# A fused attention kernel on one core: copies one step later, a longer routing tail, and the two evacuations of transposed rows moved from ScalarE to VectorE

## The chip, the core and the metric

The kernel runs on one NeuronCore of a Trainium2 chip. The metric is the device time of one launch in microseconds (us). The engines are PE (TensorE), DVE (VectorE), ACT (ScalarE), POOL (GpSimd) and SP (SyncE, which here only issues DMAs). Each runs its own list of instructions in order, and they meet only through semaphores.

## What is computed

Sixteen images of 256 rows with 77 text rows each go through a small transformer block. Cut to what matters:

```python
h = clip(sum(abs(conv2x2(x))), 0, 1)                  # 256 image rows of 256
h = concatenate([h, take(weight, x_txt)], axis=1)      # + 77 text rows: S = 333
n = layernorm(h)
q, k, v = n @ Wq + bq, n @ Wk + bk, n @ Wv + bv        # 16 heads of 16
# windows of 128 rows at stride 64 (4), and a last one: 5 windows
probs = softmax(q_w @ k_w.T * scale + pos_bias)        # per head and window, 128 x 128
merged = scatter_add(probs @ v_w) / counts
h = h + merged @ Wo + bo
x = layernorm(h)
scores, sel = top_k(softmax(x @ gate_w.T), 2)          # 8 experts, 2 for each row
out = h + sum_k(scores * (silu(x @ w1[e]) * (x @ w3[e])) @ w2[e])
```

## The kernel before

The first part (the first 830 us or so of the span) goes over the images with `run_steps`, `b` from -2 to 17. Each engine's `step(b, par)` unrolls `G` = 20 small steps `k` (5 windows of 4 groups, a group being 4 heads). In step `k` of image `b`:

- PE computes the scores of group `k` (L1026), transposes the probabilities of group `k-3` (L1040) and multiplies those of group `k-4` with v (L1063).
- DVE adds the bias and takes the row minimum (L757), ACT takes the exponent (L622), and the transposed probabilities are copied out of `t_bank` by ACT (L636, three groups of four) or DVE (L772, the fourth). `probs` has 4 buffers, `probsT` and the score bank 2.

Between these, at numbers of `k` written out by hand on every engine, stands the work for other images: projection for image `b+1` (`proj`), input and first layernorm of `b+2` (`inp`), output projection, second layernorm and transposes of `b-1` (`tail`), and the routing to experts of `b-2` (`tail2`). Since each engine is in order, a place in this order decides what waits behind what.

The projection matters most. ACT writes q and k to `qk` (L660). Each is then split in three bf16 parts: DVE makes the first (`part_high`, L733), POOL the remainder (`split_rest`, L502), DVE the second (`part_middle`, L738), POOL the third (`split_last`, L507). The argument 0 is q, 1 is k. SP writes the parts to DRAM (`write_part`, L366) and reads them back six times over as the stacks from which the scores are computed (`load_stack`, L372: 6 DMAs for q, 6 for k, 166.5 KB each). SP's order, for the projection of image `b+1`, is written out: the parts q0, k0, q1, q2, k1 (10 DMAs), then the q stack, then k2 (2 DMAs), the store of h, the k stack, and the four shifts of v. The k stack waits until all parts of k have landed. PE's first score matmul of the next image waits for both stacks.

The routing ends in six scatters of rows into expert regions (`scatter`, L493), issued from POOL.

The second part (from about 883 us on) is the expert stage, 91 tiles.

Of the kernel before, what the change touches and what calls it, by code (L numbers as in the profile page):

```python
# [29 lines left out]
GH = 4  # L30
# [28 lines left out]
def build(nc, x, x_txt, table, Wq, bq, Wk, bk, Wv, bv, Wo, bo, pos_bias, gate_wT, w1, w2, w3, use, out):  # L59
    ctx = ExitStack()  # L60
    with ctx:
# [72 lines left out]
        probsT = sb("probsT", [P, 2, GH * WIN])  # L134
# [182 lines left out]
        def _(sp):  # L317
# [17 lines left out]
            def step(b, par):  # L335
# [24 lines left out]
                if proj:  # L360
# [49 lines left out]

            sp.wait_ge(wo_done, B * 2)
# [24 lines left out]
        def _(pool):  # L436
# [50 lines left out]
            def step(b, par):  # L487
# [22 lines left out]
                for k in range(G):  # L510
                    v = (k - 5) // NG
                    if (k - 5) % NG == 3 and ((att and v >= 0) or (tail and v < 0)):
# [9 lines left out]
                    if inp and k == 0:  # L522
                        pool.wait_ge(idx_in, b2 * 16 + 16)
# [3 lines left out]
                        pool.indirect_dma_start(h_in[par][0:TXT, 2, :], None, table,  # L527
                                                bass.IndirectOffsetOnAxis(text_idx[0:TXT, 0:1], 0)).then_inc(text_in, 16)
                    if inp and k == 2:
                        pool.wait_ge(x_in, b2 * 64 + 64)  # L530
                        if b2 >= 1:
                            pool.wait_ge(image_ready, b2)
                        pool.tensor_tensor(diag[:, :, :], x_here[:, :, 0:IMG], x_below[:, :, 1:IMG + 1],
                                           ALU.subtract).then_inc(diffs_ready, 1)
                    if inp and k == 3:
                        pool.tensor_tensor(anti[:, :, :], x_below[:, :, 0:IMG], x_here[:, :, 1:IMG + 1],
                                           ALU.subtract).then_inc(diffs_ready, 1)
                    if tail2 and k == 4:
# [4 lines left out]
                    if proj and k == 5:  # L543
                        split_rest(0)
                    if tail2 and k == 5:
                        scatter(0, 1)
                    if tail2 and k == 6:
                        scatter(0, 2)
# [680 lines left out]
```

## Time and profile before

| | us |
|---|---|
| median of 3 runs (1399.01 to 1402.45) | 1400.3 |
| the profiled execution, its own time | 1394.69 |
| its span, first to last instruction | 1392.9 |
| PE busy, share of the span | 1189.1, 85% |
| DVE busy | 920.9, 66% |
| ACT busy | 782.9, 56% |
| POOL busy | 611.8, 44% |
| mean granted TensorE clock | 0.919 |

The shares are means over two stages with different limits. In the expert stage, from 883 us on, PE is busy 496 of 500 us and the change touches nothing. The images before that are the part to read, and there all engines but POOL are busy most of the time, so that the order decides.

### The profile page before, as it was taken

Reading aid. Unit: us, or ns where it says so; the run is one execution under the profiler, and the core shown is the slowest. Engines: PE = TensorE matmul, PEld = TensorE weight load, DVE = VectorE, ACT = ScalarE, POOL = GpSimd, SP = SyncE. Lnnn points to the kernel's source line nnn. Section 1 sums busy time; section 2 is a strip of 40 time slices with the busy share of each in tenths; the row PEclk is TensorE's granted clock in tenths of the full one; section 3 lists DMA queues with packets and bytes.
Section 4 is the critical chain, followed back from the end, with each engine's and each line's share of the span. In section 5 each row is a group of like instructions: output and inputs, shape, how many; then the busy total and the mean of one; then the engine's idle time right before and its main releaser. Section 6 shows DMA issues by size and latency. Waiting matters only on the chain.

```text
span 1392.9 us, 35049 instructions
## 1 busy us (share of the span) xinstructions
PE 1189.1 (85%) x10190; PEld 951.8 (68%) x10191; DVE 920.9 (66%) x4211; ACT 782.9 (56%) x3176; POOL 611.8 (44%) x900
## 2 busy tenths in 40 slices
PE   2386888988988998888889872999999999999996
PEld 1254656655655665555556551999999999999995
DVE  4485989888888889898997864344444444444442
ACT  0196998989899998899899980211111111111110
POOL 5333466565646655665665334122322232232232
PEclk9698899889898988999998985899999999999998
DMA  3694563465357446634643507232233323323222
GB/s 110 133 234 100 109 132 89 95 131 113 88 103 142 92 92 116 128 89 94 133 107 71 96 24 234 36 50 46 49 47 48 49 45 49 48 46 48 46 49 31
DMA packets 98402, 123.36 MB, mean 89 GB/s; under 512 B 15544, under 2 KB 87416, under 8 KB 95192
## 3 DMA queue, kind: packets, MB, share of 16 engines
q1 hardware_dynamic: 75880, 89.96, 30.6%
q0 software_dynamic: 18576, 24.47, 10.9%
q10 hardware_dynamic: 3808, 7.34, 1.8%
q8 instruction: 57, 0.93, 0.3%
q14 instruction: 81, 0.66, 0.2%
HBM read 69.35 MB, written 46.07 MB: 83 GB/s over the span
## 4 chain that ended last, share of the span: by engine, by line
PE 47%; POOL 16%; issue 14%; DMA 12%; ACT 4%; SPq 3%; DVE 3%; POOLq 0%; DVEq 0%; ACTq 0%
PE s_bank L1168 12%; PE t_bank L1168 12%; PE o_bank L1183 11%; DMA qk_parts<-parts_flat 5%; POOL expert_slots L493 4%; DMA expert_slots<-rows,slot_i 4%; DMA stacks<-qk_parts 3%; PE m_bank L1104 3%; ACT probs L622 3%; PE t_bank L1040 2%; SPq L372 2%; POOL rest L502 2%; PE o_bank L1063 2%; POOL parts_flat L507 2%; PE m_bank L1157 1%
## 5 line engine op out<-in xcount | busy, mean ns | idle before, releaser
L622 ACT ACTIVATE probs<-probs,neg_max 128x128 f32<-128x128 f32 x1280 | 497.4, 401 | 21.6 <-DVE neg_max L757 21.0
L757 DVE CUSTOM_DVE_ANT_0 probs<-s_bank,nbias 128x128 f32<-128x128 f32 x1280 | 293.0, 284 | 38.4 <-PE s_bank L1026 36.9
L622 ACT ACTIVATION_READ_ACCUMULATOR probs<-probs,neg_max 128x1 f32 x1280 | 257.4, 201 | 0.0
L1040 PE MATMUL t_bank<-ident,probs 128*128 128x128 f32 x1280 | 221.0, 300 | 28.7 <-ACT probs L622 26.7
L681 ACT ACTIVATE v_all<-s_bank 128x512 f32<-128x512 f32 x91 | 54.4, 598 | 286.9 <-PE s_bank L1168 286.9
L1026 PE MATMUL s_bank<-stacks 96*128 96x128 bf16 x1280 | 136.5, 233 | 68.8 <-DMA stacks<-qk_parts 46.9
L1026 PEld LDWEIGHTS s_bank<-stacks 96*128 96x128 bf16 x1280 | 93.4, 105 | 132.4 <-DMA stacks<-qk_parts 50.7
L1040 PEld LDWEIGHTS t_bank<-ident,probs 128*128 128x128 f32 x1280 | 150.1, 153 | 45.7 <-ACT probs L622 41.7
L636 ACT ACTIVATE probsT<-t_bank 128x512 f32<-128x512 f32 x240 | 141.9, 591 | 57.5 <-PE t_bank L1040 56.7
L1183 PE MATMUL o_bank<-stacks,v_all 128*128 x728 | 172.6, 380 | 0.7 <-issue 0.5
L597 POOL DMA_INDIRECT out_dram<-wq_sb,nbias x46 | 75.7, 1645 | 198.5 <-DVE wq_sb L967 185.3
L1063 PE MATMUL o_bank<-probsT,v_all 128*32 128x128 f32 x2560 | 146.0, 303 | 16.9 <-ACT probsT L636 9.7
L597 POOL DMA_INDIRECT out_dram<-wk_sb,nbias x45 | 73.3, 1629 | 172.8 <-DVE wk_sb L967 170.0
L973 DVE TENSOR_TENSOR v_all<-v_all,t_bank 128x512 f32<-128x512 f32 x91 | 62.6, 688 | 127.1 <-PE t_bank L1168 127.1
L1183 PEld LDWEIGHTS o_bank<-stacks,v_all 128*128 128x128 f32 x728 | 131.3, 190 | 16.0 <-issue 1.8
L675 ACT ACTIVATE v_all<-m_bank 128x256 f32<-128x256 f32 x91 | 35.0, 384 | 143.3 <-PE m_bank L1157 143.3
L493 POOL DMA_INDIRECT expert_slots<-rows,slot_i x96 | 100.0, 1042 | 29.3 <-issue 21.7
L1063 PEld LDWEIGHTS o_bank<-probsT,v_all 128*32 128x32 f32 x2560 | 52.9, 112 | 79.0 <-issue 50.0
L757 DVE DVE_READ_ACCUMULATOR2_ANT neg_max<- 128x1 f32 x1280 | 103.8, 81 | 0.1
L1168 PEld LDWEIGHTS s_bank<-v_all,probs 128*128 128x128 f32 x736 | 91.0, 195 | 3.2 <-ACT v_all L675 0.9
L1168 PE MATMUL s_bank<-v_all,probs 128*128 128x128 f32 x736 | 91.4, 278 | 0.5 <-ACT v_all L675 0.5
L1168 PE MATMUL t_bank<-v_all,probs 128*128 128x128 f32 x736 | 90.7, 277 | 0.0
(158 smaller groups left out, 2079.4 us busy)
## 6 DMA issues: line engine op xcount, KB each, us to landing
stacks<-qk_parts SPq DMA_DIRECT2D x192, 166.5 KB, 5.6
qk_parts<-parts_flat SPq DMA_DIRECT2D x192, 83.2 KB
nbias<-expert_slots SPq DMA_DIRECT2D x91, 129.0 KB, 2.0
w_sb<-in_L_ffn_w_dram ACTq DMA_DIRECT2D x14, 512.0 KB, 5.2
v_all<-v_all SPq DMA_DIRECT2D x64, 96.0 KB, 6.4
x_here<-in_x_dram SPq DMA_DIRECT2D x16, 256.0 KB, 5.7
out_dram<-h_res SPq DMA_DIRECT2D x16, 256.0 KB
stacks<-in_L_ffn_w_dram SPq DMA_DIRECT2D x8, 512.0 KB, 8.5
```

The costliest lines, as they stand in the source:

```text
L493: pool.indirect_dma_start(slots_dram[:, :], bass.IndirectOffsetOnAxis(slot_i[0:n, kk, j:j + 1], 0), rows[0:n, kk, j, :], None).then_inc(sc ...
L597: pool.indirect_dma_start(out[:, :], bass.IndirectOffsetOnAxis(g_rows[r][:, D + 1:D + 2].bitcast(I32), 0), y_sb[r], None, compute_op=ALU.a ...
L622: ins = act.activation(seg, seg, ACT.Exp, bias=neg_max[:, r, i:i + 1], scale=-1.0, accum_out=row_sum[:, (par + v) % 2, h:h + 1])
L636: act.activation(probsT[:, k % 2, :], t_bank[:, k % 2, :], ACT.Copy).then_inc(pT_by_act, 1)
L681: act.activation(hidT[r % 2], s_bank[:, r % 2, :], ACT.Silu).then_inc(silu_ready, 1)
L757: ins = dve.tensor_tensor_reduce(probs[:, r, i * WIN:(i + 1) * WIN], s_bank[:, k % 2, i * WIN:(i + 1) * WIN], nbias[:, h, :], 1.0, BIG, AL ...
L973: dve.tensor_tensor(hidT[r % 2], hidT[r % 2], t_bank[:, r % 2, :], ALU.mult).then_inc(hid_ready, 1)
L1026: mm = pe.matmul(s_bank[:, k % 2, i * WIN:(i + 1) * WIN], q_stack[par][0:KROWS, h, lo:lo + WIN], k_stack[par][0:KROWS, h, lo:lo + WIN], st ...
L1040: mm = pe.transpose(t_bank[:, (k - 3) % 2, i * WIN:(i + 1) * WIN], probs[:, r, i * WIN:(i + 1) * WIN], ident[:, :])
L1063: mm = pe.matmul(o_bank[32 * i:32 * i + 32, vp, (g // 2) * WIN:(g // 2 + 1) * WIN], v_win[bp][:, w, c0:c0 + 2 * HD], probsT[:, (k - 4) % 2 ...
L1168: mm = pe.matmul(bank[:, par, n * P:(n + 1) * P], up_w[par][:, m, a, n * P:(n + 1) * P], gxT[par][:, a * P:(a + 1) * P], start=(a == 0), s ...
L1183: mm = pe.matmul(o_bank[:, r % 2, 0:D], hidT[r % 2][:, a * P:(a + 1) * P], w2_sb[:, bass.ds(e, 1), a, :].rearrange("p o n -> p (o n)"), st ...
```

## The change

The step numbers move on all engines, two buffers are added, and some work changes its engine.

- Later copies: ACT copies the transposed probabilities of group `k-3` in step `k`, ahead of that step's exponent; before it was group `k-2`, behind it. The product with v moves from `k-4` to `k-6`. `probsT` has 4 buffers, two of them in the room of expert 6's `w3`, whose load moves to the end of the images.
- Longer tail: the output projection moves from steps 6 and 7 to 10 and 11, the transposes before the gate from 16 to 18, the gate matmuls from 18 to step 3 of the next image, and all that follows them likewise; the scatters from POOL's steps 4 to 9 to its steps 11 to 13.
- The v projection moves from 10 and 11 to 6 and 7. The first layernorm's statistics move from 15 to 5, its inverse root (POOL) from 16 to 12, and its normalisation from 18 to 16. The sum and clamp of the convolution move from DVE (step 11) to POOL (step 3).
- The two evacuations of transposed rows, `xT` and `x2T` (128x666 each, out of `m_bank`), move from ACT to DVE.
- The splits: `part_high` from DVE's steps 4 and 6 to 5 and 7, `part_middle` from 6 and 8 to 8 and 10, `split_last` of k from POOL's step 9 to 10.
- SP: the v shifts stand ahead of the k stack, and the store of h behind it.

```diff
+        probsT2 = sb("probsT", [P, 2, GH * WIN])
+        probsT = [probsT2[:, i, :] for i in range(2)] + [w3_sb[:, E - 2, c, :] for c in range(C)]
...
-                    if tail:
-                        store_h2()
-                    load_stack(1, k_stack[par1], K_SLOTS)
...
+                    load_stack(1, k_stack[par1], K_SLOTS)
+                    if tail:
+                        store_h2()
...
+                        act.activation(probsT[n % 4], t_bank[:, n % 2, :], ACT.Copy).then_inc(pT_by_act, 1)
...
-                        act.activation(xT[:, :, :], m_bank[:, :, 0:S], ACT.Copy).then_inc(xT_ready, 1)
...
+                        dve.tensor_copy(xT[:, :, :], m_bank[:, :, 0:S]).then_inc(xT_ready, 1)
...
-                        act.activation(x2T[:, :, :], m_bank[:, :, 0:S], ACT.Copy).then_inc(x2T_ready, 1)
...
+                        dve.tensor_copy(x2T[:, :, :], m_bank[:, :, 0:S]).then_inc(x2T_ready, 1)
...
-                    if proj and k == 8:
+                    if proj and k == 10:
                         part_middle(1)
```

SP's order, for one image in the middle of the program. Before:

```order
L366 DMA qk_parts<-parts_flat 8x16x333 x10
L372 DMA stacks<-qk_parts 16x5328 x6
L366 DMA qk_parts<-parts_flat 8x16x333 x2
L357 DMA out_dram<-h_res 128x2x256
L358 DMA out_dram<-h_res 77x256
L372 DMA stacks<-qk_parts 16x5328 x6
```

And in the change:

```order
L367 DMA qk_parts<-parts_flat 8x16x333 x10
L373 DMA stacks<-qk_parts 16x5328 x6
L367 DMA qk_parts<-parts_flat 8x16x333 x2
L390 DMA v_all<-v_all 64x384
...
L394 DMA v_all<-v_all 64x384
L373 DMA stacks<-qk_parts 16x5328 x6
L358 DMA out_dram<-h_res 128x2x256
```

The last of the ten writes still waits for `part_middle` of k, and all twelve stack loads still stand behind it; only the store and the shifts have changed places.

DVE, the stretch that ends with `part_middle` of k. Before, steps 6 to 8 (the score minima L757 between them left out):

```order
L733 CAST parts_flat<-qk 128x2x333
L738 CAST parts_flat<-rest 128x2x333
...
L851 TENSOR_SCALAR diag<-diag 128x512
L851 TENSOR_SCALAR anti<-anti 128x512
...
L784 TENSOR_TENSOR head_out<-o_bank,weightT 128x256
L856 SCALAR_TENSOR_TENSOR h_res<-m_bank,inv_count,h_res 128x256 x2
L856 SCALAR_TENSOR_TENSOR h_res<-m_bank,inv_count,h_res 77x256
L738 CAST parts_flat<-rest 128x2x333
```

In the change, steps 8 to 10 (the score minima L770 left out):

```order
L739 CAST parts_flat<-rest 128x2x333
L746 TENSOR_TENSOR v_all<-m_bank,bv_row 128x8x2x16 x2
...
L845 TENSOR_TENSOR place<-o_bank,region_end 128x24
...
L859 CAST slot_i<-slot_f 128x6
L746 TENSOR_TENSOR v_all<-m_bank,bv_row 128x8x2x16
...
L830 TENSOR_REDUCE score_sum<-score_e 128x3
...
L837 TENSOR_TENSOR rows<-score_e,score_inv 128x3x2
L739 CAST parts_flat<-rest 128x2x333
```

The last cast, on which SP waits, has moved behind two more groups of minima, and v's additions and the end of the routing stand ahead of it.

POOL, the scatters of one image. Before:

```order
L520 TENSOR_TENSOR w_sb<-w_sb,head_out 128x2x128
L493 DMA expert_slots<-rows,slot_i 43776x258
L502 TENSOR_TENSOR rest<-qk,parts_flat 128x666
L493 DMA expert_slots<-rows,slot_i 43776x258 x3
L507 TENSOR_TENSOR parts_flat<-rest,parts_flat 128x2x333
L502 TENSOR_TENSOR rest<-qk,parts_flat 128x666
```

And in the change:

```order
L510 TENSOR_TENSOR parts_flat<-rest,parts_flat 128x2x333
L505 TENSOR_TENSOR rest<-qk,parts_flat 128x666
L510 TENSOR_TENSOR parts_flat<-rest,parts_flat 128x2x333
L539 TENSOR_TENSOR ctxT<-ctxT,head_out 128x2x128
L496 DMA expert_slots<-rows,slot_i 43776x258 x3
L475 TENSOR_SCALAR var_eps<-moments 128x3
```

The scatters no longer stand among the splits; all six are issued after `split_last` of k.

## Rows read from the trace of the kernel before

**Rows 1.** Windows: one image, us busy of each engine, clock, DMA share, GB/s.

```profile
440.06:487.94 47.88, 41.80 (x399) 28.69 (x398) 42.00 (x240) 43.02 (x188) 28.46 (x50) 0.89 0.53 109
```

**Rows 2.** Timeline of PE: the first score matmuls of images 1, 7, 8, 15.

```profile
116.21 0.61 PE L1026 MATMUL s_bank<-stacks 96*128 96x128 bf16 x4 [12.46 <-DMA stacks<-qk_parts]
...
400.63 0.61 PE L1026 MATMUL s_bank<-stacks 96*128 96x128 bf16 x4 [1.36 <-DMA stacks<-qk_parts]
...
449.23 0.61 PE L1026 MATMUL s_bank<-stacks 96*128 96x128 bf16 x4 [2.06 <-DMA stacks<-qk_parts]
...
786.04 0.61 PE L1026 MATMUL s_bank<-stacks 96*128 96x128 bf16 x4 [1.73 <-DMA stacks<-qk_parts]
```

**Rows 3.** Timeline of SP's queue: part writes and stack loads, issue times.

```profile
415.30 12.49 SPq L366 DMA_DIRECT2D qk_parts<-parts_flat  x10
427.89 2.72 SPq L372 DMA_DIRECT2D stacks<-qk_parts  x6
...
438.98 4.10 SPq L372 DMA_DIRECT2D stacks<-qk_parts  x6
```

**Rows 4.** Timeline of DVE: normalisation, a first minimum, the last middle part.

```profile
399.78 2.56 DVE L714 TENSOR_SCALAR xn<-h_in,moments,rstd 128x256 f32<-128x256 f32 x3 [2.10 <-POOL rstd L484]
...
403.94 0.27 DVE L757 CUSTOM_DVE_ANT_0 probs<-s_bank,nbias 128x128 f32<-128x128 f32 x1
...
425.65 0.92 DVE L738 CAST parts_flat<-rest 128x666 bf16<-128x666 f32 x1 [0.37 <-POOL rest L502]
```

**Rows 5.** Timeline of PE: score matmuls of steps 5, 8 and 9, gate matmuls.

```profile
414.36 0.39 PE L1026 MATMUL s_bank<-stacks 96*128 96x128 bf16 x4
...
421.91 0.39 PE L1026 MATMUL s_bank<-stacks 96*128 96x128 bf16 x4
...
423.03 0.40 PE L1026 MATMUL s_bank<-stacks 96*128 96x128 bf16 x4
...
444.25 1.33 PE L1142 MATMUL o_bank<-gate_sb,rest 128*128 128x8 f32 x12
```

**Rows 6.** Windows of DVE over three routing pieces: choice, payload, places.

```profile
405.11:406.61 1.50, 1.40 (x8) 0.50 0.00 0
410.36:411.02 0.66, 0.62 (x8) 1.00 0.00 0
411.85:412.79 0.94, 0.84 (x8) 1.00 0.00 0
```

**Rows 7.** Groups by line: busy us, mean ns of one, idle before.

```profile
L757 DVE CUSTOM_DVE_ANT_0 probs<-s_bank,nbias 128x128 f32<-128x128 f32 x1280 | 293.0, 284 | 38.4 <-PE s_bank L1026 36.9 <-issue 1.1
L772 DVE COPY probsT<-t_bank 128x512 f32<-128x512 f32 x80 | 53.2, 665 | 29.2 <-PE t_bank L1040 28.7
L738 DVE CAST parts_flat<-rest 128x666 bf16<-128x666 f32 x32 | 19.0, 595 | 3.9 <-POOL rest L502 3.9
L745 DVE TENSOR_TENSOR v_all<-m_bank,bv_row 128x256 f32<-128x256 f32 x48 | 18.5, 414 | 0.0
L706 DVE BATCH_NORM_STATS2 stats<-h_res 128x6 f32<-128x256 f32 x48 | 17.1, 409 | 0.0
...
L636 ACT ACTIVATE probsT<-t_bank 128x512 f32<-128x512 f32 x240 | 141.9, 591 | 57.5 <-PE t_bank L1040 56.7
```

**Rows 8.** Timeline of DVE and POOL: a weight copy and a split.

```profile
428.04 1.87 DVE L776 COPY weight<-inv_sum 128x256 f32<-128x256 f32 x1
428.34 1.41 POOL L507 TENSOR_TENSOR parts_flat<-rest,parts_flat 128x666 bf16<-128x666 f32 x1
```

**Rows 9.** Windows of the scatters (DMA share is the last but one).

```profile
415.00:427.90 12.90, 12.08 (x118) 8.18 (x117) 10.25 (x55) 12.51 (x57) 11.45 (x11) 1.00 0.33 94
```

**Rows 10.** The chain that ended last: the last scatter's landing.

```profile
429.95 8.31 DMA expert_slots<-rows,slot_i
```

**Rows 11.** Timeline of POOL: an inverse root starts, what follows it.

```profile
443.80 0.23 POOL L472 TENSOR_SCALAR var_eps<-moments 128x3 f32<-128x3 f32 x1
...
447.61 1.80 POOL L586 TENSOR_TENSOR h_res<-h_in,bo_row 128x768 f32<-128x768 f32 x1
```

More of the change, by code:

```diff
@@ L567, in step @@
                         inverse_root(moments2, rstd2, root2_step, b0, rstd2_ready)
-                    if tail and k == 15:
+                    if tail and k == 18:
                         pool.wait_ge(rows0_ready, b0 * 3 + 3)
@@ L613, in step @@
                 for k in range(G):
+                    g = (k - 3) % NG
+                    if g != 3 and ((k >= 3 and att) or (k < 3 and tail)):
+                        n = b * G + (k - 3)
+                        act.wait_ge(pT_done, n + 1)
+                        if n >= 4:
+                            act.wait_ge(pv_done, n - 3)
+                        act.activation(probsT[n % 4], t_bank[:, n % 2, :], ACT.Copy).then_inc(pT_by_act, 1)
                     if (k >= 1 and att) or (k < 1 and tail):
@@ L749, in step @@
                 for k in range(G):
+                    v = (k - 7) // NG
+                    if (k - 7) % NG == 0 and ((att and v >= 0) or (tail and v < 0)):
+                        n, wv, vp = b * G + (k - 4), b * NW + v, (par + v) % 2
+                        dve.wait_ge(pT_done, n + 1)
+                        if n >= 4:
+                            dve.wait_ge(pv_done, n - 3)
+                        dve.tensor_copy(probsT[n % 4], t_bank[:, n % 2, :]).then_inc(pT_by_dve, 1)
+                        dve.wait_ge(inv_ready, wv + 1)
+                        if wv >= 2:
+                            dve.wait_ge(weightT_done, wv - 1)
+                        dve.tensor_copy(weight[:, vp, :, :], inv_sum[:, vp, :].unsqueeze(2).to_broadcast([P, H, HD]))\
+                            .then_inc(weight_ready, 1)
                     if att:
@@ L806, in step @@
                             .then_inc(taken_ready, 1)
-                    if tail2 and k == 2:
+                    if tail2 and k == 10:
                         dve.wait_ge(score_e_ready, b9 + 1)
@@ L851, in step @@
                             dve.tensor_scalar(bits, bits, 0x7FFFFFFF, None, ALU.bitwise_and).then_inc(conv_step, 1)
-                    if tail and k == 8:
+                    if tail and k == 12:
                         dve.wait_ge(wo_done, b0 * 2 + 2)
@@ L859, in step @@
                                                      op0=ALU.mult, op1=ALU.add).then_inc(h2_ready, 1)
-                    if proj and k == 8:
+                    if proj and k == 10:
                         part_middle(1)
-                    if tail and k == 10:
+                    if tail and k == 13:
                         dve.wait_ge(h2_ready, b0 * NT + NT)
@@ L881, in step @@
                         add_v(1, 2)
-                    if proj and k == 14:
+                    if proj and k == 9:
                         add_v(2, 4)
-                    if tail and k == 14:
+                    if tail and k == 17:
                         dve.wait_ge(rstd2_ready, b0 + 1)
```

268 lines of the change are left out of this document (124 added, 144 removed).

## The prediction, made before the changed kernel was run

> **What bounds the kernel now.** I read the windows first, then the timelines of PE, DVE and SP's queue around the start of an image. In one image of 47.88 us PE is busy 41.8, DVE 42.0 and ACT 43.0 us [rows 1]. No engine is full, three are close to it, and about 5 us per image are lost to waits. The first score matmuls of images 1 and 15 start at 116.21 and 786.04 us [rows 2]: 14 periods of 47.85 us. That period is what the change can move. The expert stage and the start stay as they are.
>
> Every first score matmul of an image in these rows waited for a DMA: 1.36, 2.06, 1.73 us [rows 2]. So I followed that DMA back. The ten part writes end at 415.30 + 12.49 = 427.79, the q stack's loads follow at 427.89, the k stack's loads wait until 438.98 for the parts of k to land [rows 3], and PE starts at 449.23. What released the last of the ten writes is DVE's `part_middle` of k, which ended at 425.65 + 0.92 = 426.57 [rows 4]. This is a loop from image to image:
>
> - from the first score matmul (400.63) to the end of `part_middle` of k (426.57): 25.9 us, work of PE and DVE in their order;
> - from there to the next first score matmul (449.23): 22.7 us, nearly all of it DMA.
>
> Together 48.6 us, which is this image's own period. The loop is not alone: DVE was late at the same place. It stood idle 2.10 us for the inverse root and took 2.56 us for three normalisations, so that the first minimum of the image came only at 403.94, 3.3 us after its matmul started [rows 4]. The DMA part thus has some 2 us to spare today, no more.
>
> **The change, part by part.** In the second half of the loop nothing gets shorter. SP still sends ten writes, six loads, two writes, then waits. The v shifts (4 x 96 KB) take the place of the store (333 KB) in the 11 us of waiting ahead of the k stack, a like amount. I keep 22.7 us; the bounds are 21.4 (427.79 to 449.23, as though the last write came free) and 22.7 plus what the scatters add. They now start after `split_last` of k, beside the q and k stack loads. Five scatters and ten writes of parts together took 0.33 x 12.9 = 4.3 us of all 16 DMA engines [rows 9], so six scatters are worth at most about 3 us, of which those two that already ran beside the loads are a third: 0 to 2 us more. I take 0.5.
>
> The Trainium skill's page "DMA: Bandwidth & Descriptors", section "Queues, rings and completion order", says that each DMA engine goes round the queue rows that have work, packet by packet. This agrees with the last scatter, which took 8.31 us to land beside the stack loads [rows 10]. By that rule the scatters would take their full share of the loads' time, and the sum would stand at its upper bound of 2 us rather than at 0.5.
>
> The first half of the loop gets longer, because `part_middle` of k goes from DVE's step 8 to step 10, and more work is put ahead of it. PE first. Score matmuls of step 5 began 414.36 - 400.63 = 13.7 us into the image, those of step 8 at 21.3 us, a bare step takes 423.03 - 421.91 = 1.1 us [rows 5]. PE was packed in that stretch, so the gate matmuls that now stand in step 3 add their 1.2 to 1.3 us [rows 5]; the v projection replaces the output projection (12 matmuls each, even). Step 5 then has its scores at 13.7 + 0.4 + 1.2 = 15.3 us.
>
> Then DVE, in order, from there to `part_middle` of k (steps 5 to 10):
>
> - six groups of minima, 293.0 us / 320 groups = 0.92 each [rows 7]: 5.5;
> - three statistics (17.1 / 48 each) [rows 7]: 1.1, and their three aggregates, some 0.2;
> - the three pieces of routing, 1.5 + 0.66 + 0.94 [rows 6]: 3.1;
> - one copy of transposed probabilities, 0.67 [rows 7], and one weight copy, 0.25 to 1.87 [rows 8], taken as 0.3;
> - four casts (two high, two middle) at 0.5 to 0.6 [rows 7]: 2.1;
> - three additions of v's bias at 0.39 [rows 7]: 1.1;
> - two reciprocals with their head products, about 0.55 together: 1.1.
>
> That is 15.2 us, and the end is at 15.3 + 15.2 = 30.5 us where it was 25.9. I take 30.3. The lower bound is PE's path alone: step 10's scores at 21.3 + 1.2 + 2 x 1.1 + 0.4 = 25.1, and step 10's own DVE work (0.92 + 0.55 + 0.66 + 0.5 = 2.6) behind it, 27.7 us. The upper bound has two weight copies at 1.9 in place of 0.3, 33.5 us.
>
> A weight copy of 1.87 us began just ahead of a POOL split of 1.41 us and ended just behind it [rows 8]. The Trainium skill's page "SBUF — State Buffer", section "SBUF: two separate sides", has the pair of ports shared by VectorE and GpSimd as an exclusive lock for a whole instruction. The trace agrees here. The rule speaks for one part of the change: the normalisation at step 16 has no large POOL add beside it, and should fall from 2.56 to about 1.2 us; but this saving stands in DVE's tail, not in the loop.
>
> The evacuations: ACT loses two of 0.72 us per image, DVE gains two. Both bounds from the 512-column copy: 0.67 on DVE against 0.59 on ACT [rows 7], so 0.7 to 0.9 us each. DVE gives the convolution's sum and clamp to POOL (0.7 + 0.4). ACT's 43.0 us become about 41.7, DVE's stay near 42 to 43. If the loop were not there, this together with the later copies could bring the period to 44 or 45 us. The later copies and the extra buffers take short waits away from PE and ACT, but those waits are not what closes the loop.
>
> Sum: 30.3 + 22.7 + 0.5 = 53.5 us per image against 47.85, 5.65 us more, in 14 periods +79 us. The first images and the expert stage count as even: the first periods wait for the expert weights' loads anyway (12.46 us at image 1 [rows 2]), the last image may win 2 us and the longer tail lose as much. From the execution's own 1394.7 this gives 1474; the median of the runs stands 5.6 us above it, so the prediction for the median is 1480.
>
> **The rivals.**
>
> *It gets faster, at 1350 to 1390.* The mechanism is the later copies: with two more steps of room the engines pack better, and the late inverse root of DVE is gone. For it: the 2.10 us of idle time and the 1.3 us of slow normalisation [rows 4] really disappear, and ACT loses 1.3 us. Against: it decides only if `part_middle` of k ends less than 47.85 - 22.7 = 25.2 us after the first score matmul, and PE's path alone needs 27.7. It could be if the DMA half shrinks by 3 us as well. A period of 45.5 gives 1400 - 33 = 1367.
>
> *No change.* Both halves at their lower bounds are 27.7 + 21.4 = 49.1 us, still +18 us; a tie needs both to be missed a little.
>
> *It is slower, but by DVE and not by the DMA.* The engines overlap better in the first half than I add up, the stacks come in time, and DVE with 43 us of work plus its lock waits sets a period of 49 to 50.5: 1416 to 1437. PE would then not wait longer than 2 us for the stacks.
>
> *It is slower still: the scatters come back as a wait.* The second normalisation overwrites the rows that are scattered, and waits until the six scatters have landed. They now start some 2.5 us after `part_middle` of k, three of them behind an inverse root of 3.8 us [rows 11]. The last is issued about 13 us after it, at 43 us, and lands 5 to 8 us later [rows 10], at 48 to 51 us; DVE would come there at about 42 us. DVE then stands idle up to 9 us, of which the DMA half of the loop hides all but 1 to 3. Period 55 to 57.5, time 1500 to 1535.
>
> **How the numbers follow.** My forecast, a period of 51 to 55 us by the DMA loop (1440 to 1500), has 0.56. The scatters' wait (1500 to 1535) 0.17. DVE's own limit (1405 to 1440) 0.13. No change 0.04, faster 0.10. A measurement of this kernel can tell about 0.3%, 4 us. So faster 0.10, same 0.04, slower 0.86. The range is 1415 to 1535: it leaves out faster and same (0.14) and the edges of the other cases (some 0.05).
>
> **What would show it.** In the changed profile the first score matmul of every image should wait 4 to 8 us for the stacks, where it was 1.4 to 2.1; `part_middle` of k should end near 30 us after it; from there to the next first matmul it should be 22.5 to 24 us. ACT's busy time per image should fall by 1.3 us and its idle time rise. The normalisation at step 16 should wait for no inverse root. I am wrong if `part_middle` of k ends at 26 us or less, or if the DMA half turns out below 20 us: then what I called fixed was queueing that the new order removes. I am wrong in size if DVE stands waiting for scatters.

## The result, and the profile after

The change made the kernel slower: 1447.8 us (median of 4 runs, 1444.9 to 1454.4) against 1400.1 us (4 runs, 1399.0 to 1402.5), a ratio of 1.0345 with the interval 1.0306 to 1.0384. I had predicted 1480 us in a range of 1415 to 1535. The direction was right, the time lies in the case that I held likeliest (1440 to 1500), and the size was 1.7 times too large (+48 us where I had summed +80). That case's main mark, long waits for the stacks, was missing.

The windows view of one image after the change (from one first score matmul to the next) answers to [rows 1]. Its columns are busy time and count of PE, PE's weight loads, DVE, ACT and POOL, then granted clock, share of the DMA engines, GB/s:

```profile
422.81:473.05 50.24, 43.25 (x403) 29.93 (x399) 41.26 (x239) 41.94 (x186) 28.92 (x52) 0.87 0.47 103
```

This image takes 50.24 us where that one took 47.88 (over thirteen images, from 120.13 to 780.04 us, the period is 50.76). ACT and DVE have less to do than before, so neither has become the limit; the image got longer around them. PE's timeline shows the first score matmuls of the image, as in [rows 2] and [rows 5]:

```profile
422.81 0.61 PE L1030 MATMUL s_bank<-stacks 96*128 96x128 bf16 x4
...
425.19 0.39 PE L1030 MATMUL s_bank<-stacks 96*128 96x128 bf16 x4
...
426.59 0.39 PE L1030 MATMUL s_bank<-stacks 96*128 96x128 bf16 x4
...
428.93 0.39 PE L1030 MATMUL s_bank<-stacks 96*128 96x128 bf16 x4
...
432.49 0.38 PE L1030 MATMUL s_bank<-stacks 96*128 96x128 bf16 x4
...
434.83 0.39 PE L1030 MATMUL s_bank<-stacks 96*128 96x128 bf16 x4
...
469.88 1.37 PE L1134 MATMUL m_bank<-ident,rows 128*128 128x128 f32 x6 [2.64 <-DVE rows L715]
...
473.05 0.61 PE L1030 MATMUL s_bank<-stacks 96*128 96x128 bf16 x4
```

Steps 0 to 5 start at 0, 2.4, 3.8, 6.1, 9.7 and 12.0 us; I had put step 5 at 15.3. Then PE's wait is not where I expected it. The first score matmul of the next image (473.05) waits for nothing; PE has already lost 2.64 us at 469.88, before the transposes of the normalised rows, which DVE delivered late.

DVE's timeline, from the scores of step 5 to the middle part of k (the row of [rows 4] that closed the first half), and then the two normalisations:

```profile
435.26 0.29 DVE L770 CUSTOM_DVE_ANT_0 probs<-s_bank,nbias 128x128 f32<-128x128 f32 x1 [0.57 <-PE s_bank L1030]
...
445.88 1.40 DVE L851 TENSOR_TENSOR place_k<-onehot,place 128x48 f32<-128x48 f32 x1
...
449.82 0.51 DVE L739 CAST parts_flat<-rest 128x666 bf16<-128x666 f32 x1
...
463.35 1.08 DVE L715 TENSOR_SCALAR xn<-w_sb,moments,rstd 128x256 f32<-128x256 f32 x3
468.76 1.06 DVE L715 TENSOR_SCALAR rows<-h_res,moments,rstd 128x256 f32<-128x256 f32 x3 [2.87 <-POOL rstd L487]
```

Before, the middle part of k ended 25.9 us after the first score matmul; now it is 450.33 - 422.81 = 27.5 us. The normalisation of xn takes 1.08 us and waits for nothing, where it had waited 2.10 and taken 2.56. The other one waits 2.87 us; the row names POOL's inverse root, which was done 0.67 us before.

SP's queue, for [rows 3]:

```profile
436.71 14.83 SPq L367 DMA_DIRECT2D qk_parts<-parts_flat  x10
451.65 2.71 SPq L373 DMA_DIRECT2D stacks<-qk_parts  x6
454.40 1.22 SPq L367 DMA_DIRECT2D qk_parts<-parts_flat  x2
...
462.83 3.93 SPq L373 DMA_DIRECT2D stacks<-qk_parts  x6
```

The q stack follows the middle part by 1.3 us, as before, and the k stack follows the q stack by 11.2 us (11.1 before). From its issue to the next first score matmul it is 10.2 us, again as before, though PE came there without a wait for the stacks.

POOL's timeline between the last split of k and the second inverse root's end:

```profile
450.41 1.41 POOL L510 TENSOR_TENSOR parts_flat<-rest,parts_flat 128x666 bf16<-128x666 f32 x1 [3.19 <-DVE parts_flat L739]
451.77 0.78 POOL L539 TENSOR_TENSOR w_sb<-w_sb,head_out 128x256 f32<-128x256 f32 x1
452.72 1.04 POOL L496 DMA_INDIRECT expert_slots<-rows,slot_i  x1 [0.16 <-issue]
...
456.40 0.23 POOL L475 TENSOR_SCALAR var_eps<-moments 128x3 f32<-128x3 f32 x1
...
463.07 0.96 POOL L496 DMA_INDIRECT expert_slots<-rows,slot_i  x1 [0.30 <-issue]
464.10 0.38 POOL L475 TENSOR_SCALAR var_eps<-moments 128x3 f32<-128x3 f32 x1
...
467.89 0.20 POOL L487 TENSOR_TENSOR rstd<-rstd,root_tmp 128x3 f32<-128x3 f32 x1
```

Here is something that the prediction had only as a side branch. From 450.41 to 468.09 POOL pauses nowhere for more than 0.4 us: split, one addition, three scatters, the first inverse root (3.8 us), three scatters, the second root (4.0 us). Only then, and when the scatters have landed, can DVE normalise, PE transpose, and the image end. This chain starts from the same middle part of k that starts the DMA chain, and ends within a few us of the same place.

### The profile page after: what moved, and what is told of

Same layout as the page of the kernel before. It is cut to its first block, busy times and chain, and to the rows that moved or that the text cites. A ratio compares the mean times of both kernels' runs of the same rounds, so it can differ in the third digit from the quotient of the medians.

```text
span 1447.4 us, 35047 instructions
## 1 busy us (share of the span) xinstructions
PE 1194.6 (83%) x10190; PEld 963.6 (67%) x10191; DVE 902.9 (62%) x4211; ACT 763.3 (53%) x3144; POOL 629.0 (43%) x932
## 3 DMA queue, kind: packets, MB, share of 16 engines
q0 software_dynamic: 18576, 24.47, 10.8%
## 4 chain that ended last, share of the span: by engine, by line
PE 40%; issue 3%; ACT 3%; DVE 2%; POOL 2%; SPq 1%; DMA 1%; another core or an unknown queue 1%; POOLq 0%; DVEq 0%; ACTq 0%
PE s_bank L1168 11%; PE t_bank L1168 11%; PE o_bank L1183 11%; ACT probs L638 2%; PE m_bank L1157 1%; PE t_bank L1044 1%; PE o_bank L1067 1%; POOL expert_slots L496 1%; PE m_bank L1108 1%; PE s_bank L1030 1%; DMA stacks<-qk_parts 1%; PE o_bank L1142 0%; DVE probs L770 0%; PE m_bank L1008 0%
## 5 line engine op out<-in xcount | busy, mean ns | idle before, releaser
L770 DVE CUSTOM_DVE_ANT_0 probs<-s_bank,nbias 128x128 f32<-128x128 f32 x1280 | 292.8, 284 | 146.2 <-PE s_bank L1030 131.7
L1044 PE MATMUL t_bank<-ident,probs 128*128 128x128 f32 x1280 | 227.1, 306 | 67.8 <-ACT probs L638 62.3
L638 ACT ACTIVATION_READ_ACCUMULATOR probs<-probs,neg_max 128x1 f32 x1280 | 252.6, 197 | 0.0
L1044 PEld LDWEIGHTS t_bank<-ident,probs 128*128 128x128 f32 x1280 | 154.9, 157 | 86.1 <-ACT probs L638 76.3
L1030 PEld LDWEIGHTS s_bank<-stacks 96*128 96x128 bf16 x1280 | 99.3, 106 | 103.6 <-DMA stacks<-qk_parts 52.7
L629 ACT ACTIVATE probsT<-t_bank 128x512 f32<-128x512 f32 x160 | 94.7, 592 | 91.6 <-PE t_bank L1044 83.7
L496 POOL DMA_INDIRECT expert_slots<-rows,slot_i x96 | 96.6, 1006 | 37.9 <-issue 28.9
L770 DVE DVE_READ_ACCUMULATOR2_ANT neg_max<- 128x1 f32 x1280 | 104.0, 81 | 0.1
L510 POOL TENSOR_TENSOR parts_flat<-rest,parts_flat 128x666 bf16<-128x666 f32 x32 | 45.2, 1413 | 110.5 <-DVE parts_flat L739 110.5
L1168 PEld LDWEIGHTS s_bank<-v_all,parts_flat 128*128 128x128 f32 x720 | 87.4, 192 | 3.0 <-ACT v_all L676 0.7
```

Of the source, the lines that this page charges most:

```text
L496: pool.indirect_dma_start(slots_dram[:, :], bass.IndirectOffsetOnAxis(slot_i[0:n, kk, j:j + 1], 0), rows[0:n, kk, j, :], None).then_inc(sc ...
L510: pool.tensor_tensor(parts[:, 2 * n:2 * n + 2, 2, :], rest[:, :, :], parts[:, 2 * n:2 * n + 2, 1, :], ALU.subtract).then_inc(part3_ready, 1)
L629: act.activation(probsT[n % 4], t_bank[:, n % 2, :], ACT.Copy).then_inc(pT_by_act, 1)
L638: ins = act.activation(seg, seg, ACT.Exp, bias=neg_max[:, r, i:i + 1], scale=-1.0, accum_out=row_sum[:, (par + v) % 2, h:h + 1])
L770: ins = dve.tensor_tensor_reduce(probs[:, r, i * WIN:(i + 1) * WIN], s_bank[:, k % 2, i * WIN:(i + 1) * WIN], nbias[:, h, :], 1.0, BIG, AL ...
L1030: mm = pe.matmul(s_bank[:, k % 2, i * WIN:(i + 1) * WIN], q_stack[par][0:KROWS, h, lo:lo + WIN], k_stack[par][0:KROWS, h, lo:lo + WIN], st ...
```

## The experiments

The hypothesis after the trace (theory A): two loops from image to image share their first half. The first half ends with DVE's middle part of k. One second half goes over SP's writes and stack loads to the first score matmul ("the DMA loop", the one predicted). The other goes over POOL's split, scatters and two roots to DVE's second normalisation and PE's transposes ("the POOL loop"). Both take about 50 us, so shortening one alone shows little. The rivals: the DMA loop alone, the POOL loop alone, or DVE's own work.

All twelve runs, with the two kernels compared. In the runs' own series the kernel before took 1397 to 1399 us. The period is worked out: the mean distance of DVE's residual additions (the row `h_res` with scalar_tensor_tensor) over the twelve images from the second to the fourteenth. "Low clock" is (1 - mean granted clock) x 2 x span, the time that TensorE spent at the lower of its two levels, 0.50 in the rows or 1.2 GHz.

| kernel | us | ratio to before, interval | period | low clock |
|---|---|---|---|---|
| before | 1400 | 1 | 48.0 | 226 |
| after | 1448 | 1.0345 (1.0306 to 1.0384) | 50.9 | 278 |
| a_split | 1424 | 1.0180 (1.0137 to 1.0223) | 50.4 | 217 |
| a_root | 1450 | 1.0379 (1.0333 to 1.0424) | 51.6 | 253 |
| a_both | 1367 | 0.9801 (0.9766 to 0.9835) | 44.9 | 130 |
| b_split | 1425 | 1.0208 (1.0174 to 1.0242) | 49.6 | 270 |
| a_short | 1426 | 1.0196 (1.0179 to 1.0213) | 50.7 | 217 |
| a_root_short | 1368 | 0.9780 (0.9763 to 0.9798) | 45.4 | 148 |
| a_act | 1451 | 1.0381 (1.0364 to 1.0398) | 51.4 | 232 |
| c_act | 1373 | 0.9836 (0.9789 to 0.9884) | 45.9 | 137 |
| c_mom | 1476 | 1.0550 (1.0507 to 1.0594) | 53.5 | 297 |
| c_sp | 1424 | 1.0182 (1.0160 to 1.0203) | 49.5 | 225 |
| c_short | 1425 | 1.0198 (1.0181 to 1.0216) | 49.6 | 222 |
| b_dve | 1445 | 1.0341 (1.0307 to 1.0375) | 51.4 | 271 |

### The later splits alone, in the kernel before

The kernel before with the change's steps for the casts and splits of q and k, and nothing else (the edit's core on DVE; POOL's `split_rest` and `split_last` move by one step in the same way):

```
-                    if proj and k == 4:
+                    if proj and k == 5:
                         part_high(0)
-                    if proj and k == 6:
+                    if proj and k == 7:
                         part_high(1)
-                        part_middle(0)
-                    if proj and k == 8:
+                    if proj and k == 8:
+                        part_middle(0)
+                    if proj and k == 10:
                         part_middle(1)
```

> The kernel before with one part of the change: its casts and splits at the steps of the changed kernel (high parts in DVE's steps 5 and 7, middle parts in 8 and 10, POOL's splits in 6, 8 and 10). Nothing else moves. The DMA loop: its first half grows from 25.9 us by the two steps' work on DVE, about 4 us, of which some 2 us were spare; period 47.85 + 2 to 4 us, 1400 + 28 to 56 = 1428 to 1456, and PE waits 4 us or more for the stacks at every image. If the DMA loop does not matter (DVE's late inverse root and POOL set the period): no change, 1400.

Measured: 1424.6 us, 3 us under the range, period 49.6. The waits of this kernel between 250 and 800 us (line, what it waited for, us in total, times, longest):

```profile
PE s_bank L1027 <- DMA stacks<-qk_parts: 50.3, 11, 5.5
...
DVE xn L714 <- POOL rstd L484: 25.0, 11, 2.3
```

PE now stands 50.3 us in 11 images at the first score matmul, waiting for the stacks, up to 5.5 us. That is the wait that the prediction described, in the frame of the kernel before. The middle part of k ends 27.2 us into the image (mean of images 4 to 14; 25.9 in the kernel before), and from there to the next image it is 22.5 us. The later splits alone are enough for +28 us (+2.1%) through the DMA.

### The splits back, the root earlier, and both, in the kernel after

a_split puts the casts and splits of the kernel after back into the steps of before (the reverse of the edit above). a_root moves one block of POOL's:

```
+                    if inp and k == 7:
+                        ...
+                        inverse_root(moments1, rstd1, root1_step, b2, rstd1_ready)
                     if proj and k == 8:
                         split_last(0)
                         split_rest(1)
                     ...
-                    if inp and k == 12:
-                        ...
-                        inverse_root(moments1, rstd1, root1_step, b2, rstd1_ready)
```

a_both has both (its root stands in step 9, behind `split_last(1)`, which that kernel reaches earlier).

(The first four expectations number the theories: the third there is the two loops of about the same length, the theory A of this text.)

> The changed kernel with one part undone: the casts and splits stand at the steps of the kernel before (high parts in DVE's steps 4 and 6, middle parts in 6 and 8, POOL's splits in 5, 7 and 9). In the changed kernel the first score matmul of an image to the end of the last middle part is 27.5 us, and 22.7 us more to the next image. Theory 1, the DMA loop alone sets the period: the first half falls by the 5.6 us that step 8's place is earlier, the period from 50.8 to about 45.5 us, and the time from 1448 to 1375. Theory 2, the chain over POOL alone sets it (scatters, inverse root, scatters, inverse root, second normalisation, transposes, next image): POOL's last split no longer stands right ahead of the scatters, which may start 2.4 us earlier, so 1448 - 14 x 2.4 = 1414. Theory 3, both close at the same length: also about 1414, with PE waiting for normalised rows and no more for the stacks.

> The changed kernel with the first layernorm's inverse root moved from POOL's step 12 (between the two halves of the scatters) to step 7, where POOL stands idle for 4.3 us waiting for a middle part. The second inverse root then comes 3.9 us earlier after the scatters. Theory 1 (DMA loop alone): no change, 1448, and PE waits for the stacks in nearly every image. Theory 2 (POOL chain alone): the wait of 3 to 4 us ahead of the second normalisation goes, about 3 us per image, 1448 - 42 = 1406. Theory 3 (both at the same length): 0.5 us per image, 1441, and the wait of PE moves from normalised rows to the stacks.

> The changed kernel with both: the casts and splits at the steps of the kernel before, and the first inverse root in POOL's step 9, behind the last split and ahead of the scatters. Theory 3 (both loops at the same length): only now does the period fall freely, to 45 to 46.5 us, 1448 - 14 x 5 = 1378, faster than the kernel before (1400). Theory 1 alone: as with the split steps alone. Theory 2 alone: as with the inverse root alone, 1406.

Measured: 1424, 1450 and 1367 us. a_split gained 24 us, but its period fell by only 0.5 us; the larger part came from the last three images (from the first score matmul of image 13 to the expert stage 185.9 us, where the kernel after took 199.4). What holds it is in its waits:

```profile
DVE rows L715 <- issue: 71.4, 11, 7.8
...
PE m_bank L1133 <- DVE rows L715: 64.7, 11, 7.2
```

DVE waits 6.5 us per image before the second normalisation, and PE behind it nearly as long (5.9 us): the middle part of k now ends 22.5 us into the image instead of 27.9 (means of eleven images), but the other loop is as long as before.

What DVE waits for there is not the root. "Issue" says that the profile shows no releaser. The last row of the root and DVE's first row behind it, in one image:

```profile
462.57 0.19 POOL L487 TENSOR_TENSOR rstd<-rstd,root_tmp 128x3 f32<-128x3 f32 x1
...
465.11 1.06 DVE L715 TENSOR_SCALAR rows<-h_res,moments,rstd 128x256 f32<-128x256 f32 x3 [6.25 <-issue]
```

The root is done at 462.76, 2.35 us before DVE starts (2.2 to 3.9 us in the eleven images). In the code this normalisation waits for three things: the root, PE's transposes of an image ago, and the landing of the six scatters. So it is the scatters that are left, and the last packet of their queue ended 0.5 to 1.2 us before DVE started. In the kernel after the root was done 0.7 to 2.6 us earlier in six of eleven images, and 0.03 us earlier in the other five. So the POOL loop often ends with the landing of the scatters, and not with the root; theory A had only the root there. This is read from the traces and the code, no run separates it. In a_root the same wait is still there, and the wait for the stacks has come back:

```profile
DVE rows L715 <- issue: 38.4, 10, 5.0
...
PE s_bank L1030 <- DMA stacks<-qk_parts: 28.4, 11, 4.4
```

The root was done 0.7 to 3.6 us before DVE started, in all eleven images. The two-loop theory had given the root alone a few us; it gave nothing. It was right that PE's wait would move to the stacks. Both together gave 80 us, far more than the sum of the two, and a kernel 2.0% faster than the one before. The waits of a_both:

```profile
PE m_bank L1133 <- DVE rows L715: 13.8, 11, 2.9
...
DVE rows L715 <- POOL rstd L487: 10.7, 9, 1.6
```

### The same crossing with shorter loads

If the two-loop picture is right, the DMA loop can be shortened in another way with the same outcome. In a_short, from the third image on, the last three of the six loads of each stack move one row of sixteen (so the scores are not the reference's):

```
                         for s, part in enumerate(slots):
-                            sp.dma_start(dst[s * HD:(s + 1) * HD, :, :], parts_dram[n, part, :, :, :])\
+                            few = 1 if b1 >= 2 and s >= 3 else HD
+                            sp.dma_start(dst[s * HD:s * HD + few, :, :], parts_dram[n, part, 0:few, :, :])\
                                 .then_inc(stack_in, 16)
```

> The kernel after the change; from the third image on, loads 4 to 6 of each stack move one row of their sixteen (so those rows of the stacks hold an older image's numbers, and the scores are not the reference's). That shortens the DMA loop alone: I estimate 3 to 5 us per image from the 10 us between the issue of the k stack and the next first score matmul. Theory A (two loops of about the same length, the DMA loop and the one over POOL's inverse roots and scatters): the POOL loop still holds, 1430 to 1450. Rival (the DMA loop alone is the bound, as the prediction had it): 14 x 3 to 5 us less, 1380 to 1405. Rival B (the POOL loop alone): nothing, 1445 to 1450.

> The kernel after the change with the first inverse root in POOL's step 7, before the first of the last splits, and the shortened stack loads of the run a_short (the last three loads of each stack move one row of their sixteen). Theory A: both loops are now shorter, so what the inverse root alone did not give comes out, 1380 to 1410. Rival B (POOL's scatters and not the root hold the rows back, whatever the DMA loop does): about 1440 to 1450, as with the root alone. Rival C (the DMA loop alone): the same time as a_short.

Measured: 1426 and 1368 us. Alone, the shorter loads left the period at 50.7 (after: 50.9) and won their 22 us at the first and the last images. Their waits:

```profile
PE m_bank L1135 <- DVE rows L716: 54.9, 11, 6.1
...
DVE rows L716 <- issue: 32.1, 6, 6.3
```

With the root moved as well, the period is 45.4. So the root's place, worth nothing alone (1450 against 1448), is worth 58 us once the loads are short, and the loads, worth 22 us alone, are worth 82 us once the root is early. "The DMA loop alone" and "the POOL loop alone" each fail at one side of this square. That the gain (5 us per image) is larger than either edit shortens by itself was not in theory A. A part of it is in the traces: the shorter loads do not shorten the DMA loop alone. The last packet of the scatters' queue ended 4.1 to 5.5 us behind POOL's last scatter in a_root, and 1.7 to 2.6 us behind it in a_root_short, where DVE then waited for the root. So this edit made the other loop shorter too, and the square does not keep the two apart as cleanly as it was meant to.

### The two evacuations

a_act is the kernel after with both copies on ACT again, c_act the same in a_both, b_dve the kernel before with both copies on DVE (in its steps 1 and 17).

```
+                    if proj and k == 0:
+                        act.wait_ge(xT_done, b1 + 1)
+                        ...
+                        act.activation(xT[:, :, :], m_bank[:, :, 0:S], ACT.Copy).then_inc(xT_ready, 1)
...
-                    if proj and k == 1:
-                        dve.wait_ge(xT_done, b1 + 1)
-                        ...
-                        dve.tensor_copy(xT[:, :, :], m_bank[:, :, 0:S]).then_inc(xT_ready, 1)
```

> The kernel after the change with the two evacuations of transposed rows back on ScalarE (in its steps 0 and 18). Theory A: the two copies lie in neither half of a loop that DVE bounds, so 1435 to 1452. Rival: DVE is the limit over the whole image, so its 1.7 us per image come back in full, 15 x 1.7 = 25 us, 1420 to 1425.

> The run a_both (casts and splits in the steps of before, first inverse root in POOL's step 9; 1367 us) with the two evacuations back on ScalarE. Both loops are loose there (45 us per image), so DVE's own work should count more. Theory A: up to 1.7 us per image comes back, 1342 to 1367. Rival (the evacuations on DVE are what made a_both faster than the kernel before): 1380 to 1400.

> The kernel before with the two evacuations of transposed rows alone moved to VectorE (its steps 1 and 17). By the DMA loop that bounds that kernel, they cost only what lies in it: the copy of xT stands in step 1, in the first half of the loop, which DVE's work fills, so 0.85 us per image, and the copy of x2T up to as much: 1397 to 1420. Rival (they take load off a late ScalarE): 1385 to 1395.

Measured: 1451, 1373 and 1445 us. In the kernel after the place of the copies makes no difference (1.0381 against 1.0345, intervals that overlap), and in a_both none either (1373 against 1367, intervals that overlap). In the kernel before, the move alone costs 46 us, 3.4%, which I had put at 0 to 20. Its trace says where: PE's projection of q waits for the copy, 2.5 us per image, which is most of the 3.5 us by which the period grew.

```profile
PE m_bank L1104 <- DVE xT L780: 27.4, 11, 3.0
```

DVE's timeline of the same image shows what stands ahead of the copy:

```profile
430.48 0.63 DVE L762 COPY probsT<-t_bank 128x512 f32<-128x512 f32 x1
431.02 1.48 DVE L766 COPY weight<-inv_sum 128x256 f32<-128x256 f32 x1
432.43 0.84 DVE L780 COPY xT<-m_bank 128x666 f32<-128x666 f32 x1
```

In the order of before, a copy of transposed probabilities and a weight copy stand in DVE's step 1, and the copy of xT comes last, while PE has stopped at 430.5 (its next row, the projection of q, starts at 433.32). With q late, everything of the first half is late. In the kernel after, the later copies have left that step, and the copy of xT (0.85 us at 426.47) follows the minima of its step directly and is done before PE projects q at 427.70. So the evacuations on DVE seem to be free only together with the later copies; that last point is read from the two timelines, no run separates it.

### What a_both owes its speed to

Three kernels take one thing away from a_both, or shorten it further. c_mom puts the statistics of the first layer norm, its root and the normalisation of xn back into the steps of before (DVE 15, POOL 16, DVE 18). c_sp gives SP the order of before, stores of h2 and k stack ahead of the shifts of v. c_short has the shortened loads of a_short.

```
# c_mom
-                    if inp and k == 5:
+                    if inp and k == 15:
                         dve.wait_ge(image_ready, b2 + 1)
# c_sp
+                    if tail:
+                        store_h2()
+                    load_stack(1, k_stack[par1], K_SLOTS)
                     vt = v_win[par1]
                     ...
-                    load_stack(1, k_stack[par1], K_SLOTS)
-                    if tail:
-                        store_h2()
```

> The run a_both with the first layer norm's statistics, its inverse root and the normalisation of xn in the steps of before (DVE 15, POOL 16, DVE 18). Theory A says nothing of the splits here, which stay early; it says that in POOL's order the root then stands behind both the scatters and the second root, and that DVE waits for it again as in the kernel before (2.1 us per image there): 1385 to 1410. Rival (the early statistics are worth nothing, and a_both beats the kernel before by its other moves): 1365 to 1372.

> The run a_both with SP's order of before: the stores of h2 and the k stack ahead of the four shifts of v. The wait of SP's queue for v is short (v is ready 4 us after the q stack in the kernel after), and the stores wait for h2 of step 12. If the change's order is what keeps the stores off the k stack's path, 1375 to 1400 (up to 2 us per image); if SP has nothing to wait for either way, 1362 to 1372. I hold the second for likelier.

> The run a_both with the shortened stack loads of a_short (three of each stack's six move one row of their sixteen from the third image on). If the DMA loop is what bounds a_both at its 45 us per image, the 1.7 us per image that the shortening gave the loop in a_short, or more, come out: 1325 to 1350. Rival (a_both is bound by DVE or by the loop over POOL): 1358 to 1372.

Measured: 1476, 1424 and 1425 us. All three missed, and c_short missed in sign: shorter loads made a_both 58 us slower. Theory A has no room for that. In c_sp and c_short both loops are loose: in images 4 to 14 (counted from 0) PE never waits for the stacks, nor DVE before the second normalisation. Something else sets their periods of 49.5 and 49.6 us. So the theory explains the square above, and is not the whole account. The waits of c_short:

```profile
DVE probs L771 <- PE s_bank L1030: 73.8, 76, 2.5
ACT weightT L654 <- remote: 64.1, 12, 5.6
...
DVE probs L771 <- remote: 31.1, 10, 5.3
```

"Remote" says that the trace shows no event on this core that released the wait. These rows come from one place in each image, between PE's scores of steps 14 and 16. ACT and DVE stand still there for up to 5.6 and 5.3 us. In a_both no such row exists. c_mom has the same rows, and its PE timeline shows what PE did meanwhile:

```profile
462.27 0.43 PE L1066 MATMUL o_bank<-w_sb,v_all 128*32 128x128 f32 x8
...
462.90 0.39 PE L1029 MATMUL s_bank<-stacks 96*128 96x128 bf16 x4
...
465.19 0.27 PE L1066 MATMUL o_bank<-probsT,v_all 128*32 128x128 f32 x1 [0.77 <-issue]
...
466.59 0.31 PE L1066 MATMUL o_bank<-probsT,v_all 128*32 128x128 f32 x2 [0.43 <-issue]
467.32 0.30 PE L1066 MATMUL o_bank<-probsT,v_all 128*32 128x128 f32 x2 [0.42 <-issue]
...
468.23 0.38 ACT L653 ACTIVATE weightT<-o_bank 128x256 f32<-128x256 f32 x1 [4.74 <-remote]
...
469.02 0.61 PE L1029 MATMUL s_bank<-stacks 96*128 96x128 bf16 x4 [0.73 <-DVE neg_max L770]
```

Eight of these matmuls take 0.43 us in the step before; here one or two are issued every 0.7 us, and step 15's scores (469.02) come 6.1 us after step 14's (462.90).

The distance from the scores of step 14 to those of step 16 measures the stall. In images 4 to 14 it is 3.7 to 3.8 us in every image of a_both, a_root_short and c_act, but also of the slow a_split, a_root, a_act and a_short. It is 9.2 to 10.1 us in every image of c_sp and c_short, 9.4 to 9.7 in c_mom, and 4.7 to 11.4 (mean 6.3) in the kernel after. So the stall adds some 6 us to each image of the three. It accounts for c_sp and c_short whole: up to step 14 an image takes 32.1 us there (a_both 31.6), then 6 us more than in a_both, and behind step 16 it is 1.9 us shorter, together 4.7 us per image. In c_sp the wait for the store costs the k stack nothing (11.0 us behind the q stack, 10.8 in a_both), so my reading of SP's queue was right, and the time came from the stall; what ties the stall to SP's order is not shown. c_mom has the stall and, besides, the late DVE at the start of the image that I had expected there: step 1's scores come at 6.3 us, in a_both at 2.4.

What holds PE there stays open. POOL's scatters run through the same stretch, but they do in a_both as well. Packets of the two instruction queues come up to 23 us apart in the traces, and none of them starts in the stalls of c_mom (464 to 468) or c_short (444 to 448, 494 to 498).

## Why the prediction was right, and where it was off

**What bounded the kernel before** was read rightly in the main. b_split moves only what was said to close the loop, and the time goes up by 28 us with 50.3 us of waits for the stacks in eleven images. But the sentence that every first score matmul "in these rows" waited for a DMA rests on chosen rows: of images 5 to 15 of that trace, three did not wait and one waited 0.06 us.

**The second half** (22.7 + 0.5 = 23.2 us) measured 22.7 in this image, where PE did not wait for the stacks, so its end was set by the other chain. A better measure is the two runs in which PE waited for the stacks in all eleven images: 22.5 us on average in b_split, with the scatters at their places of before, and 22.7 in a_root, with them beside the loads. The term was right, and the scatters added some 0.2 us to the loads. By the Trainium skill's round of the queues ("DMA: Bandwidth & Descriptors", "Queues, rings and completion order") I had put it at up to 2 us more; these traces do not show that.

**The first half** (30.3 us, where the items sum to 30.5) measured 27.5 us in this image and 27.9 on average. The mis-sized term is the sum "13.7 + 0.4 + 1.2 = 15.3" for the scores of step 5, which came at 12.0 us. I took the first steps of before as fixed. They were slow where DVE was late at the start of the image ([rows 4], 2.10 us of waiting and 2.56 of work); with that gone the first steps ran faster, and this I had counted only as two us of "room", not as a gain. c_mom shows it: it makes DVE late again in a_both, and step 5's scores come at 16.9 us instead of 12.0 (means of ten images). DVE's stretch from there to the middle part of k, summed as 15.2 us, measured 450.33 - 435.26 = 15.07 us. That total was partly luck: one addend, a routing product (445.88), took 1.40 us, as in 13 of the 16 images, where it had taken 0.2 before, and others took less.

**The sum** 27.5 + 22.7 = 50.2 us is this image's period; the mean is 50.76, and 14 periods of +2.9 us are +41. The expert stage starts 56.4 us later than before (927.6 against 871.2 us). Of the other 16 us the start cost 3.9 (120.13 against 116.21) and the last image with its routing tail 11.9 (97.0 us against 85.1), where I had put both as "even". Per image I was off by nearly a factor of two (+5.65 summed, +2.9 measured), and a term that I had put at nothing made up for part of it; that much of the closeness is luck. The spans differ by 54.5 us and the medians by 47.6, since the profiled execution of before lay some 5.5 us under its median and that of after 1.4 us above.

**The mark "the first score matmul waits 4 to 8 us for the stacks"** failed in the kernel after. The wait was there, but PE spent it earlier, at the transposes of the normalised rows (29.0 us in 11 images), so that next to nothing was left for the stacks (three waits of 0.3 to 1.1 us). The step that failed in the text is "so I followed that DMA back": I followed one chain from the middle part of k, where two leave it. My rival on the scatters saw the second ("DVE would come there at about 42 us"): its place was right, its size was not. It had DVE idle up to 9 us and a time of 1500 us or more; DVE's waits there were 2.2 to 4.9 us, and the landing of the scatters, which it named, is what is left as the last to come in six of eleven images. By setting it aside as a rival I missed that the two chains were equal, and that undoing either alone would leave the period where it was. The rival "by DVE and not by the DMA" had the mark that came true, no long wait for the stacks, but not the cause: DVE was busy only 41.26 us of this image.

**The marks that held**: ACT's busy time fell from 43.0 to 41.9 us per image (I had written -1.3), the normalisation at step 16 waits for nothing and takes 1.08 us ("about 1.2"), and `part_middle` of k ends 27.5 us into the image, above the 26 that would have refuted me, though not near the 30 that I had named.

**The rival "faster"** had asked for the middle part of k before 25.2 us, and had put 1367 us to it. a_both has it at 22.3 us and takes 1367; that the number is the same is luck. The condition is not enough: a_split has it at 22.5 us and takes 1424. Whether the later copies bring the gain, as the rival said, no run shows.

## What to carry to other kernels

When an instruction that many things wait for is moved later, list all chains that leave it, not only the one that ends last now. If two have nearly the same length, test them crossed (one, the other, both), since each alone will look worthless. And move a copy to another engine only after asking what stands ahead of it there and when its reader comes: the same two copies cost 46 us in one order and nothing in the other. And when an edit is meant to shorten one chain, look whether the other one got shorter with it.

## What the runs showed that I had not expected

**The periods fall into groups.** The kernel after and the twelve runs gave 44.9 to 45.9 us or 49.5 to 53.5 us, the kernel before 48.0, and nothing between. In the upper group different waits come last: for the stacks (b_split, a_root), for the rows of the second normalisation (a_split, a_short), and the stall of PE (c_sp, c_short). An edit that frees 2 us of a chain gave either nothing or 5 us per image.

**The clock goes with the groups.** Windows of 2 us in the kernel after show it (columns as above; of the last three numbers the first is the granted clock):

```profile
416.00:418.00 2.00, 0.95 (x12) 0.51 (x12) 0.00 (x0) 2.00 (x10) 1.50 (x6) 0.84 1.12 175
418.00:420.00 2.00, 0.37 (x2) 0.37 (x3) 1.48 (x8) 1.71 (x10) 0.36 (x1) 0.50 0.85 124
420.00:422.00 2.00, 2.00 (x14) 1.89 (x12) 2.00 (x11) 0.00 (x0) 1.20 (x2) 0.50 1.06 331
422.00:424.00 2.00, 2.00 (x18) 1.27 (x16) 1.97 (x14) 1.67 (x8) 1.80 (x1) 0.50 0.34 90
424.00:426.00 2.00, 2.00 (x28) 1.44 (x29) 0.77 (x7) 2.00 (x11) 1.10 (x2) 0.95 0.00 0
```

PE waits for the normalised rows, the granted clock drops to 0.50 (1.2 GHz), and the first steps of the next image run at that level until 424. A stretch of 50 us of a_both reads:

```profile
410.00:460.00 50.00, 42.45 (x426) 29.67 (x426) 43.83 (x264) 45.44 (x203) 31.83 (x64) 0.97 0.54 117
```

and of the kernel after:

```profile
410.00:460.00 50.00, 42.56 (x396) 29.79 (x395) 38.87 (x223) 40.88 (x181) 28.65 (x50) 0.86 0.47 101
```

The three fast kernels spent 130 to 148 us at the lower level, all others 217 to 297. A wait that slows the matmuls behind it would make small savings and losses larger, and would give such groups. That is argued from these rows only. No run separated the clock as a cause from the clock as a consequence of PE's waits, and a_split and c_sp, with as little low clock as the kernel before (217 and 225 us against 226), are 25 us slower than it, so it is not the whole account.

**A stall of PE that no row explains**, some 6 us between steps 14 and 16 in c_sp, c_short and c_mom and on average 2.6 us in the kernel after, told above. What the kernel after loses by it is not shown: a_split, a_root, a_short and a_act are free of it and have periods of 50.4 to 51.6 us.
